# First four tiles of a two-layer attention kernel: another order of work on all five engines, with two large loads moved to ScalarE's queue

## The chip, the cores and the metric

One NeuronCore of a Trainium2 chip runs the kernel alone. The metric is the device time of one execution in microseconds (us); a shorter time is better. The engines are TensorE (PE in the profile, its weight loads PEld), VectorE (DVE), ScalarE (ACT), GpSimd (POOL) and SyncE (SP), which only issues DMAs. ScalarE can issue DMAs too.

## The reference

Two layers of the same form follow each other on x of shape (32, 128, 512). Layer 0 has 16 heads, layer 1 has 8. Cut to what matters:

```python
xn = layernorm(x) * scale + bias
q, k, v = xn @ Wq + bq, xn @ Wk + bk, xn @ Wv + bv      # k and v masked along the sequence
q = softmax(q, over the channels of a head)
k = softmax(k, over the sequence)
att = einsum('bhse,bhsd->bhed', k, v)                   # per head
y = einsum('bhtd,bhed->bhte', q, att)
scale, shift = split(silu(cond) @ film_W + film_b)      # cond is (32, 1024)
h = silu(layernorm(y) * (1 + scale) + shift) @ Wo + bo
x = x + h
```

All is fp32. The kernel splits every operand of a product into a rounded high part and the rest (low part), and sums three products: high by high, high by low, low by high.

## The kernel before

A tile is one of the 64 pairs of layer and batch row (128 positions by 512 channels). Tiles are handled in pairs: `x` is normalised (`stat_x` and `root_x` for mean and deviation, `norm_x`), turned so that the channels lie on the partitions (`turn_x`), scaled (`x_turned`, which writes the high part XH too) and its low part taken (`x_low`). TensorE then makes `keys`, `values` and `queries` (48 matmuls in all), each with the weights' high parts WH (`split_high`) and low parts WL (`split_low`), chunk by chunk of 128 rows. The keys go through mask, maximum and exponential (`keys` on VectorE, `exp_k`, `key_sums`, `normalise_keys`), `attention` forms the product of keys and values, `heads` copies it out of PSUM, `mix` multiplies it with the queries' exponentials (`exp_q`), and `mixed`, `root_y`, `norm_y`, `film`, `h_mul`, `h_high`, `h_low` and `output` do the rest. `conditioning` and `conditioning_fold` make the scales and shifts of all batch rows from `cond`; `conditioning_sums` copies between the two.

For the first two pairs (tiles 0 to 3), `turn_x` is a transpose by TensorE through PSUM. From tile 4 on VectorE transposes blocks of 32 (XS), and two DMAs through DRAM finish it: `write_x` and `read_x` on SP's queue, landing in XT, which `x_turned` reads.

Every engine has its own order of work, written out by hand as a list of calls, and waits on semaphores that its producers raise. The lists of the start (tiles 0 to 4) are written out; `step(s)` repeats from s = 5. An engine does its list strictly in order, so a call that waits holds up all that stand behind it on that engine. SP's list is the order of the DMAs. Weights of layer 0 land in STAGE (keys, later output), and in tiles 8 to 11 and 12 to 15 of X (values, queries), so the loads of those tiles of x come later; the conditioning weights land in tiles 16 to 31 of X.

`keep_busy(b, n)` makes n matmuls of the identity into a PSUM bank whose content nobody reads: two records in the trace for each.

TensorE's list at the start is: 10 `keep_busy`, `turn_x(0)`, `turn_vectors`, `turn_x(1)`, 14 `keep_busy`, `keys(0)`, `keys(1)`, 2 `keep_busy`, `turn_x(2)`, `turn_valid`, `queries(0)`, `values(0)`, `queries(1)`, `turn_x(3)`, `values(1)`, `turn_cond`, `count`, `keys(2)`, `conditioning(0)`, `queries(2)`, `keys(3)`, `values(2)`, `conditioning_fold(0)`, `attention(0)`, `mix(0)`, `attention(1)`, `values(3)`, `queries(3)`, `conditioning(1)`, `mix(1)`, 5 `keep_busy`, `conditioning_fold(1)`, 2 `keep_busy`, `keys(4)`, and so on.

The lines that the prediction names: L1152 the matmuls of `split_product` (keys, values, queries, output), L1232 `attention`, L1248 `mix`, L1305 `turn_x` on TensorE, L1346 `keep_busy`, L1351 `count`; L346 `split_low`, L1575 to L1581 `keys` on VectorE, L1677 the high part of h by a VectorE copy at the end; L687 `mask_of_keys`, L667 `x_low` and L651 `add_bo` on GpSimd; L902 `heads`, L935 and L942 `x_turned`; L405 and L413 `write_x` and `read_x`, L377 and L381 the loads of x and of the weights.

Of the kernel before, what the change touches and what calls it, by code (L numbers as in the profile page):

```python
# [36 lines left out]
P = 128  # L37
# [7 lines left out]
def build_blocks(nc, x, cond, mask0, mask1, weights, film_w, vec_rows, bias_rows, out):  # L45
# [4 lines left out]
    C = D // P  # L50
# [16 lines left out]
    with ctx:  # L67
# [107 lines left out]
        act_cond, act_w = sem("act_cond"), sem("act_w")  # L175
# [164 lines left out]

        def split_low(eng, w, chunks):

            for c in chunks:
                wait_weights(eng, w, c)
                eng.wait_ge(act_w, C * w + c + 1)
                eng.tensor_tensor(WL[w % 4][:, c, :], STAGES[w][:, c, :], WH[w % 4][:, c, :].bitcast(F32),  # L346
                                  ALU.subtract).then_inc(low_w[w][c], 1)
# [26 lines left out]
        def _(eng):  # L374
# [130 lines left out]
            load_bias(2)  # L505
            load_bias(0)
            load_bias(1)
            load_w(2)
            load_film(0)
            load_x(3)  # L510
            wait_split(1)

            load_x(4)
            write_qy(1)
            load_film(1)
# [3 lines left out]
            wait_split(0)  # L519
            load_w(3)  # L520
            write_x(2)
            write_qy(2)
            read_x(2)
            read_qy(2)
            write_qy(3)
            write_x(3)
            masks_at(2)
# [73 lines left out]
        def _(eng):  # L601
# [92 lines left out]
            mask_of_keys(0)  # L694
            root_x(2)
            root_x(3)
            split_low(eng, 2, [0])
            normalise_keys(0)
            queries(0)
            root_x(4)  # L700
            mask_of_keys(1)
            normalise_keys(1)
            root_x(5)
            root_x(6)
            queries(1)
            normalise_keys(2)
            root_x(7)
            root_x(8)
            add_bo(0)
            queries(2)  # L710
            root_x(9)
            add_bo(1)
            root_y(0)
            x_low(4)
            split_low(eng, 3, [1])
            normalise_keys(3)
# [95 lines left out]
        def _(eng):  # L812
# [148 lines left out]

            eng.dma_start(VR, vec_rows).then_inc(ld_vec, 16)
            load_first(eng, [3])
            load_first(eng, [2])
            load_mask(eng, 0)
            eng.dma_start(COND, cond).then_inc(ld_cond, 16)
            eng.dma_start(MI, mask0).then_inc(ld_mask, 16)
            eng.dma_start(MF, mask1).then_inc(ld_mask, 16)
            split_high(0, [0])
            split_high(0, [1])  # L970
            split_high(0, [2])
            split_high(0, [3])
# [4 lines left out]
            cond_tanh()  # L977
            split_high(1, [2])
            split_high(1, [3])
            load_mask(eng, 1)  # L980
# [7 lines left out]
            exp_k(1)  # L988
            norm_x(4)
            exp_k(2)  # L990
            norm_x(5)
            conditioning_sums(0)
            exp_q(0)
            values(0)
            norm_x(6)
            norm_x(7)
            heads(0)
            values(1)
# [3 lines left out]
            values(2)  # L1002
            exp_k(3)
# [3 lines left out]
            heads(1)  # L1007
            exp_q(1)
# [129 lines left out]
        def _(eng):  # L1138
# [229 lines left out]
            keep_busy(B_Q, 4)  # L1368
            keep_busy(B_Q, 6)
            turn_x(0)  # L1370
            turn_vectors()
            turn_x(1)
            keep_busy(B_Q, 2)
            keep_busy(B_Q, 2)
            keep_busy(B_Q, 2)
            keep_busy(B_Q, 2)
            keep_busy(B_Q, 2)
            keep_busy(B_Q, 2)
            keep_busy(B_Q, 2)
            keys(0)  # L1380
            keys(1)
            keep_busy(B_Q, 2)
            turn_x(2)
            turn_valid()
            queries(0)
            values(0)
            queries(1)
            turn_x(3)
            values(1)
            turn_cond()  # L1390
            count()
# [9 lines left out]
            values(3)  # L1401
            queries(3)
            conditioning(1)
            mix(1)
            eng.wait_ge(dve_ka, 4)
            keep_busy(B_K, 5)
            conditioning_fold(1)
            keep_busy(B_K, 2)
# [91 lines left out]
        def _(eng):  # L1500
# [230 lines left out]

            def start():
# [46 lines left out]

            stat_x(0)  # L1780
            stat_x(1)
            norm_x(0)
            split_low(eng, 0, [0])
            norm_x(1)
            split_low(eng, 0, [1])
            split_low(eng, 0, [2])
            start_vectors()
            split_low(eng, 0, [3])
            stat_x(2)
            stat_x(3)  # L1790
            x_low(0)
# [252 lines left out]
```

## Time and profile before

| | us |
|---|---|
| median of three runs | 856.59 (856.27 to 859.33) |
| the profiled execution | 857.14 |
| its span | 855.1 |

The span is the time from the first to the last instruction in the profile. A share of busy time is taken over the whole span. The timeline of an engine lists instructions in order: start, duration, instruction, count and, in brackets, how long the engine sat idle before it and what ended that. The ends of matmuls are modelled and overlap with the next one's start, so on TensorE the starts are what counts.

### The profile page before, as it was taken

To read this page: it belongs to the slowest core of one execution; us is meant where nothing else is said; L and a number is where in the kernel's file an instruction comes from. 1 tells how busy PE (TensorE), PEld (TensorE's weight loads), DVE (VectorE), ACT (ScalarE), POOL (GpSimd) and SP (SyncE) were. 2 spreads that over 40 slices of the span, in tenths; PEclk is the share of its full clock that TensorE was granted. 3 is DMA by queue.
4 is the path that set the end of the run, shared out by engine and by line. 5 is a ranking of instruction groups with operands and counts; after the bars stand their busy time and mean duration, and the time that the engine had idled before them with its cause. 6 is when DMAs were issued, how large, how long until landed. Compare 5 with 4: busy or idle time off the path is not lost.

```text
span 855.1 us, 20095 instructions
## 1 busy us (share of the span) xinstructions
PE 838.2 (98%) x6659; PEld 719.9 (84%) x6659; DVE 679.3 (79%) x1362; ACT 603.1 (71%) x1442; POOL 548.9 (64%) x741
## 2 busy tenths in 40 slices
PE   7999999999999999999999999999999999999998
PEld 7778888888888888888878888888888888888886
DVE  6987778778788788778887887787788787787766
ACT  5376687686676776686876886776776686676665
POOL 3467766766766666766767667667667666765641
PEclk9999999999999999999999999999999999999999
DMA  8876676766667756555587556656566656566441
GB/s 309 286 225 201 201 218 199 228 216 205 195 210 208 233 197 199 179 165 175 169 247 233 185 172 200 201 180 201 179 204 201 202 186 189 178 194 211 142 160 62
DMA packets 139404, 169.81 MB, mean 199 GB/s; under 512 B 12302, under 2 KB 112006, under 8 KB 139302
## 3 DMA queue, kind: packets, MB, share of 16 engines
q1 hardware_dynamic: 138512, 167.56, 62.5%
q8 instruction: 53, 0.87, 0.4%
q10 hardware_dynamic: 790, 0.98, 0.4%
q14 instruction: 49, 0.40, 0.2%
HBM read 95.61 MB, written 72.88 MB: 197 GB/s over the span
## 4 chain that ended last, share of the span: by engine, by line
PE 83%; DMA 6%; DVE 4%; issue 2%; SPq 2%; POOL 1%; ACT 1%; DVEq 0%; POOLq 0%; ACTq 0%
PE PS L1152 72%; PE PS L1248 6%; PE PS L1232 3%; DMA X<-in_x 2%; DMA XT<-x_turned 1%; DMA x_turned<-XS 1%; DMA k_turned<-KT 1%; DMA QT<-qy_turned 1%; POOL XL L667 0%; SPq L400 0%; PE PS L1322 0%; DMA EK<-k_turned 0%; DVE BNX L1515 0%; PE PS L1276 0%; PE PS L1291 0%
## 5 line engine op out<-in xcount | busy, mean ns | idle before, releaser
L680 POOL TENSOR_TENSOR HL<-H,HH 128x512 fp32r<-128x512 f32 x60 | 77.5, 1292 | 185.3 <-ACT HH L916 185.3
L867 ACT ACTIVATE Z<-QT,FC,FA 128x128 f32<-128x128 f32 x240 | 99.0, 483 | 87.7 <-DMA QT<-qy_turned 87.7
L1152 PE MATMUL PS<-XH,WH_k 128*128 128x256 f32 x512 | 149.8, 293 | 0.7 <-DVE KN L1581 0.7
L1152 PE MATMUL PS<-XL,WH_k 128*128 128x256 f32 x512 | 144.8, 283 | 0.0
L1152 PE MATMUL PS<-XH,WL_k 128*128 128x256 f32 x512 | 144.8, 283 | 0.0
L953 ACT ACTIVATE XN<-X,NBX,RSX 128x512 f32<-128x512 f32 x60 | 48.8, 813 | 85.5 <-POOL NBX L629 85.5
L829 ACT ACTIVATE SK<-SK,KN 128x128 f32<-128x128 f32 x256 | 98.9, 387 | 10.7 <-DVE KN L1581 10.4
L1152 PE MATMUL PS<-WH_o,HH 128*128 128x512 f32 x248 | 101.3, 408 | 2.0 <-issue 1.9
L1152 PE MATMUL PS<-WH_v,XH 128*128 128x512 f32 x256 | 100.8, 394 | 0.0
L1152 PE MATMUL PS<-WH_q,XH 128*128 128x512 f32 x256 | 100.7, 393 | 0.0
L1152 PE MATMUL PS<-WL_v,XH 128*128 128x512 f32 x256 | 100.3, 392 | 0.0
L1152 PE MATMUL PS<-WL_q,XH 128*128 128x512 f32 x256 | 99.8, 390 | 0.0
L1152 PE MATMUL PS<-WH_v,XL 128*128 128x512 f32 x256 | 99.6, 389 | 0.0
L1152 PE MATMUL PS<-WH_q,XL 128*128 128x512 f32 x256 | 99.6, 389 | 0.0
L1152 PEld LDWEIGHTS PS<-XH,WH_k 128*128 128x128 f32 x512 | 97.9, 191 | 1.3 <-issue 1.1
L1152 PEld LDWEIGHTS PS<-XL,WH_k 128*128 128x128 f32 x512 | 98.2, 192 | 0.1
L1152 PEld LDWEIGHTS PS<-XH,WL_k 128*128 128x128 f32 x512 | 98.1, 192 | 0.0
L1152 PE MATMUL PS<-WL_o,HH 128*128 128x512 f32 x248 | 96.9, 391 | 0.0
L1152 PE MATMUL PS<-WH_o,HL 128*128 128x512 f32 x248 | 96.9, 391 | 0.0
L651 POOL TENSOR_TENSOR X<-X,BB 128x512 f32<-128x512 f32 x64 | 83.8, 1311 | 0.2
L667 POOL TENSOR_TENSOR XL<-XF,XH 128x512 fp32r<-128x512 f32 x60 | 78.1, 1302 | 5.2 <-issue 3.6
L674 POOL TENSOR_TENSOR SK<-SK,RE 128x512 f32<-128x512 f32 x64 | 66.8, 1044 | 19.7 <-DVE RE L1587 19.6
(171 smaller groups left out, 2106.6 us busy)
## 6 DMA issues: line engine op xcount, KB each, us to landing
qy_turned<-QS SPq DMA_DIRECT2D x60, 512.0 KB, 2.9
QT<-qy_turned SPq DMA_DIRECT2D x240, 128.0 KB, 3.1
EK<-k_turned SPq DMA_DIRECT2D x128, 128.0 KB, 2.8
x_turned<-XS SPq DMA_DIRECT2D x30, 512.0 KB, 3.3
XT<-x_turned SPq DMA_DIRECT2D x120, 128.0 KB, 3.5
k_turned<-KT SPq DMA_DIRECT2D x52, 256.0 KB, 3.8
out_x<-X SPq DMA_DIRECT2D x31, 256.0 KB, 3.2
X<-in_x SPq DMA_DIRECT2D x11, 512.0 KB, 5.3
```

The lines of the kernel that those rows point to most:

```text
L651: eng.tensor_tensor(X[:, b, :], X[:, b, :], BB[:, 2, :], ALU.add).then_inc(pool_bo, 1)
L667: eng.tensor_tensor(XL[g % 2][:, dst, :], XF0[:, :, :], XH[g % 2][:, dst, :].bitcast(F32), ALU.subtract).then_inc(pool_xl, 1)
L674: eng.tensor_tensor(sk, sk, RE[:, :].unsqueeze(2).to_broadcast([P, 4, T]), ALU.mult).then_inc(pool_kn, 1)
L680: eng.tensor_tensor(hl_of(o), h_of(o), hh_of(o).bitcast(F32), ALU.subtract).then_inc(pool_hl, 1)
L829: e = eng.activation(SK[:, p, a, :], SK[:, p, a, :], ACT.Exp, bias=KN[:, p, t, cc:cc + 1], accum_out=SE[:, p, a:a + 1])
L867: z = eng.activation(z_of(o)[:, c * P:c * P + P].rearrange("p (q n) -> p q n", q=Q), src, ACT.Identity, bias=FC[l][:, c, b:b + 1], scale=F ...
L953: eng.activation(XN[:, t, :], X[:, n % B, :], ACT.Identity, bias=NBX[:, r:r + 1], scale=RSX[:, r:r + 1]).then_inc(act_xn, 1)
L1152: mm = eng.matmul(dst, left[a](c), right[b](c), start=(c == 0 and a + b == 0), stop=(c == C - 1 and a == 1))
L1232: mm = eng.matmul(PS[f:f + 32, bank_att(j), c * P + a:c * P + a + w], vs if l == 0 else ks, ks if l == 0 else vs, start=True, stop=True, t ...
L1248: mm = eng.matmul(bank(B_Y + c // 2, (c % 2) * W, W), EQ[:, c * P:c * P + P], ATT[:, c // 2, (c % 2) * W:(c % 2 + 1) * W], start=True, sto ...
```

## The change

Nothing is computed otherwise; what changes is the order of the start, which engine does some of its steps, and how much `keep_busy` there is:

- ScalarE's queue no longer issues the mask and `cond` loads; SP does, behind the load of the values' weights. ScalarE issues instead the second conditioning load and the output weights' load (2 MB and 1 MB), after `exp_k(1)`. SP had issued them behind `write_qy(1)` and behind `place_keys(0)`.
- Two of the four high parts of the keys' weights are made by VectorE, one low part of each of the keys', values' and queries' weights moves from VectorE to GpSimd.
- `start` and `start_vectors` move to the front of VectorE's list; TensorE turns the vectors first.
- TensorE turns tiles 2 and 3 together ahead of the first projections, takes values before queries, and `conditioning(1)` before `queries(3)`.
- On ScalarE `heads(1)` and `exp_q(1)` go ahead of the copies of the output weights and of `x_turned(4)`; on GpSimd `add_bo(1)` moves behind `x_low(4)`, in front of `x_low(5)`.
- 25 `keep_busy` instead of 24 stand ahead of `keys(0)`; the other nine behind it are gone.

```diff
@@ -172,7 +172,7 @@
 pe_fold, act_cp = sem("pe_fold"), sem("act_cp")
-act_cond, act_w = sem("act_cond"), sem("act_w")
+act_cond, act_w, dve_w = sem("act_cond"), sem("act_w"), sem("dve_w")
 act_ek, act_eq, act_z, act_t = sem("act_ek"), sem("act_eq"), sem("act_z"), sem("act_t")
@@ -338,11 +338,20 @@
+def wait_high(eng, w, c):
+    if w == 0 and c >= C // 2:
+        eng.wait_ge(dve_w, c - C // 2 + 1)
+    elif w == 0:
+        eng.wait_ge(act_w, c + 1)
+    else:
+        eng.wait_ge(act_w, C * w - C // 2 + c + 1)
 def split_low(eng, w, chunks):
...
         wait_weights(eng, w, c)
-        eng.wait_ge(act_w, C * w + c + 1)
+        wait_high(eng, w, c)
         eng.tensor_tensor(WL[w % 4][:, c, :], STAGES[w][:, c, :], WH[w % 4][:, c, :].bitcast(F32),
@@ -502,29 +511,30 @@
     load_w(1)
-    load_bias(2)
+    load_mask(eng, 0)
+    eng.dma_start(MI, mask0).then_inc(ld_mask, 16)
+    eng.dma_start(MF, mask1).then_inc(ld_mask, 16)
+    eng.dma_start(COND, cond).then_inc(ld_cond, 16)
+    load_w(2)
     load_bias(0)
     load_bias(1)
-    load_w(2)
     load_film(0)
+    load_mask(eng, 1)
     load_x(3)
     wait_split(1)
     load_x(4)
     write_qy(1)
-    load_film(1)
     write_keys(0)
...
     place_keys(0)
-    wait_split(0)
-    load_w(3)
+    load_bias(2)
+    write_qy(2)
     write_x(2)
-    write_qy(2)
+    read_qy(2)
     read_x(2)
-    read_qy(2)
+    masks_at(2)
+    write_x(3)
     write_qy(3)
-    write_x(3)
-    masks_at(2)
     read_qy(3)
@@ -691,29 +701,32 @@
     root_x(1)
-    mask_of_keys(0)
+    split_low(eng, 0, [3])
     root_x(2)
     root_x(3)
+    split_low(eng, 1, [3])
+    mask_of_keys(0)
     split_low(eng, 2, [0])
+    split_low(eng, 2, [1])
     normalise_keys(0)
+    mask_of_keys(1)
     queries(0)
+    normalise_keys(1)
     root_x(4)
-    mask_of_keys(1)
-    normalise_keys(1)
     root_x(5)
+    queries(1)
     root_x(6)
-    queries(1)
     normalise_keys(2)
     root_x(7)
+    queries(2)
+    add_bo(0)
     root_x(8)
-    add_bo(0)
-    queries(2)
     root_x(9)
-    add_bo(1)
     root_y(0)
     x_low(4)
+    normalise_keys(3)
     split_low(eng, 3, [1])
-    normalise_keys(3)
+    add_bo(1)
     x_low(5)
@@ -959,25 +972,29 @@
+    def load_output():
+        for c in range(C):
+            eng.wait_ge(low_w[0][c], 1)
+        eng.dma_start(STAGE[:, :, :], weights[0][3].rearrange("(c p) n -> p c n", p=P)).then_inc(ld_w[2], 16)
+    def load_second_film():
+        l, a, k = FILM_STEPS[1]
+        eng.dma_start(FILM0[:, :, a:a + k], film_w[l].rearrange("(k p) n -> p k n", p=P)[:, :, a:a + k])                   .then_inc(ld_film[1], 16)
     eng.dma_start(VR, vec_rows).then_inc(ld_vec, 16)
+    load_first(eng, [2])
     load_first(eng, [3])
-    load_first(eng, [2])
-    load_mask(eng, 0)
-    eng.dma_start(COND, cond).then_inc(ld_cond, 16)
-    eng.dma_start(MI, mask0).then_inc(ld_mask, 16)
-    eng.dma_start(MF, mask1).then_inc(ld_mask, 16)
     split_high(0, [0])
     split_high(0, [1])
-    split_high(0, [2])
-    split_high(0, [3])
     x_turned(0)
...
     split_high(1, [1])
-    cond_tanh()
     split_high(1, [2])
     split_high(1, [3])
-    load_mask(eng, 1)
+    cond_tanh()
     split_high(2, [0])
@@ -986,26 +1003,28 @@
     exp_k(1)
+    load_second_film()
+    load_output()
     norm_x(4)
-    exp_k(2)
     norm_x(5)
     conditioning_sums(0)
+    exp_k(2)
+    values(0)
+    values(1)
     exp_q(0)
-    values(0)
     norm_x(6)
+    heads(0)
+    exp_k(3)
     norm_x(7)
-    heads(0)
-    values(1)
+    values(2)
+    heads(1)
+    exp_q(1)
     split_high(3, [0])
...
     split_high(3, [2])
-    values(2)
-    exp_k(3)
     norm_y(0)
...
     norm_x(8)
-    heads(1)
-    exp_q(1)
     x_turned(5)
@@ -1365,30 +1384,23 @@
     eng.wait_ge(pool_const, 2)
-    keep_busy(B_Q, 4)
-    keep_busy(B_Q, 6)
+    keep_busy(B_Q, 10)
+    turn_vectors()
+    keep_busy(B_Q, 1)
     turn_x(0)
-    turn_vectors()
     turn_x(1)
-    keep_busy(B_Q, 2)
-    keep_busy(B_Q, 2)
-    keep_busy(B_Q, 2)
-    keep_busy(B_Q, 2)
-    keep_busy(B_Q, 2)
-    keep_busy(B_Q, 2)
-    keep_busy(B_Q, 2)
+    keep_busy(B_Q, 14)
     keys(0)
     keys(1)
-    keep_busy(B_Q, 2)
     turn_x(2)
+    turn_x(3)
     turn_valid()
+    values(0)
     queries(0)
-    values(0)
+    values(1)
+    count()
     queries(1)
-    turn_x(3)
-    values(1)
     turn_cond()
-    count()
     keys(2)
@@ -1399,13 +1411,10 @@
     values(3)
+    conditioning(1)
     queries(3)
-    conditioning(1)
     mix(1)
-    eng.wait_ge(dve_ka, 4)
-    keep_busy(B_K, 5)
     conditioning_fold(1)
-    keep_busy(B_K, 2)
     def step(s):
@@ -1729,6 +1738,12 @@
+    def split_high(w, chunks):
+        for c in chunks:
+            wait_weights(eng, w, c)
+            eng.tensor_copy(WH[w][:, c, :], STAGES[w][:, c, :]).then_inc(dve_w, 1)
     def start():
@@ -1777,74 +1792,73 @@
+    start()
     stat_x(0)
...
     norm_x(0)
+    start_vectors()
+    norm_x(1)
+    split_high(0, [2])
+    split_high(0, [3])
     split_low(eng, 0, [0])
-    norm_x(1)
     split_low(eng, 0, [1])
     split_low(eng, 0, [2])
-    start_vectors()
-    split_low(eng, 0, [3])
+    x_low(0)
+    x_low(1)
     stat_x(2)
     stat_x(3)
-    x_low(0)
-    x_low(1)
     split_low(eng, 1, [0])
-    start_masks()
     norm_x(2)
+    split_low(eng, 1, [1])
     norm_x(3)
...
     keys(0)
-    split_low(eng, 2, [1])
+    start_masks()
     split_low(eng, 2, [2])
-    split_low(eng, 1, [3])
     split_low(eng, 2, [3])
-    split_low(eng, 1, [1])
+    start_valid()
     keys(1)
     key_sums(0)
-    queries(0)
-    stat_x(4)
     values(0)
-    turn_queries(0)
-    stat_x(5)
-    stat_x(6)
-    start()
-    start_cond()
     x_low(2)
     x_low(3)
-    start_valid()
+    queries(0)
+    start_cond()
     turn_keys(0)
     key_sums(1)
+    turn_queries(0)
+    turn_keys(1)
+    values(1)
     start_cond_turned()
     queries(1)
-    turn_keys(1)
+    stat_x(4)
+    stat_x(5)
     zero_attention()
     keys(2)
-    values(1)
     start_count()
...
     turn_x(4)
+    turn_x(5)
     key_sums(2)
-    turn_x(5)
+    stat_x(6)
+    queries(2)
     stat_x(7)
+    keys(3)
+    values(2)
     stat_x(8)
     stat_x(9)
-    queries(2)
-    values(2)
-    keys(3)
     mixed(0)
+    conditioning(0)
     turn_queries(2)
-    conditioning(0)
     turn_x(6)
+    turn_x(7)
     split_low(eng, 3, [0])
...
     split_low(eng, 3, [2])
-    turn_x(7)
-    queries(3)
     turn_keys(2)
...
     values(3)
+    queries(3)
     mixed(1)
```

## Rows read from the trace of the kernel before

**Rows 1.** The profile's page, first part: busy time by engine.
```profile
PE 838.2 (98%) x6659; PEld 719.9 (84%) x6659; DVE 679.3 (79%) x1362; ACT 603.1 (71%) x1442; POOL 548.9 (64%) x741
```
**Rows 2.** Busy time by stretch: stretch, length, engines, granted TensorE clock, DMA share, GB/s.
```profile
7.00:8.00 1.00, 0.03 (x1) 0.00 (x0) 0.00 (x0) 0.99 (x2) 0.00 (x0) 1.00 0.76 181
...
13.00:14.00 1.00, 1.00 (x6) 1.00 (x6) 0.93 (x3) 0.97 (x3) 0.28 (x2) 1.00 1.05 406
...
130.00:400.00 270.00, 269.63 (x2162) 231.53 (x2161) 216.99 (x439) 194.30 (x467) 179.38 (x243) 1.00 0.66 203
```
**Rows 3.** TensorE's timeline: start, duration, instruction, count, idle before and its releaser.
```profile
9.87 0.69 PE L1305 MATMUL PS<-ident,XN 128*128 128x128 f32 x2 [2.84 <-DVE XN L1526]
...
15.97 0.36 PE L1152 MATMUL PS<-XH,WH_k 128*128 128x256 f32 x1
...
23.01 0.50 PE L1152 MATMUL PS<-WH_q,XH 128*128 128x512 f32 x1
...
36.14 0.41 PE L1351 MATMUL PS<-VALID,H 128*128 128x32 f32 x2 [0.72 <-DVE VALID L1749]
...
50.66 0.46 PE L1232 MATMUL PS<-EK,VV 128*32 128x32 f32 x32
...
61.48 1.17 PE L1248 MATMUL PS<-ATT,EQ 128*128 128x132 f32 x8 [0.51 <-ACT EQ L847]
62.49 1.28 PE L1346 MATMUL PS<-ident 128*128 128x128 f32 x10
...
64.97 0.36 PE L1152 MATMUL PS<-XH,WH_k 128*128 128x256 f32 x1
```
**Rows 4.** L1346 by group, first in 11.7 to 13.5 us, then in 14.5 to 16.
```profile
L1346 PE MATMUL PS<-ident 128*128 128x128 f32 x9 | 2.1, 421 | 0.0
...
L1346 PE MATMUL PS<-ident 128*128 128x128 f32 x16 | 2.0, 277 | 0.0
```
**Rows 5.** VectorE's timeline around the first tile's keys.
```profile
19.12 0.69 DVE L1575 TENSOR_TENSOR SK<-PS,MB 128x512 f32<-128x512 f32 x1 [0.31 <-PE PS L1152]
...
20.57 1.02 DVE L1579 TENSOR_TENSOR KB<-KM,VC 128x4 f32<-128x4 f32 x1
```
**Rows 6.** GpSimd's timeline.
```profile
10.77 1.40 POOL L687 TENSOR_SCALAR MB<-MB 128x256 f32<-128x256 int32 x1 [4.07 <-DMA MB<-in_mask]
...
20.28 1.29 POOL L346 TENSOR_TENSOR WL_q<-X,WH_q 128x512 fp32r<-128x512 f32 x1 [4.33 <-ACT WH_q L819]
...
52.24 1.28 POOL L651 TENSOR_TENSOR X<-X,BB 128x512 f32<-128x512 f32 x1
...
59.87 1.30 POOL L667 TENSOR_TENSOR XL<-XF,XH 128x512 fp32r<-128x512 f32 x1 [3.55 <-issue]
...
63.34 1.28 POOL L667 TENSOR_TENSOR XL<-XF,XH 128x512 fp32r<-128x512 f32 x1
```
**Rows 7.** ScalarE's timeline: weight copies, first `heads`, `norm_y`, `x_turned(4)`.
```profile
19.48 2.20 ACT L819 ACTIVATE WH_q<-X 128x512 fp32r<-128x512 f32 x4 [0.87 <-DMA X<-in_wq]
...
51.20 0.60 ACT L902 ACTIVATE ATT<-PS 128x512 f32<-128x512 f32 x1 [3.20 <-PE PS L1232]
...
56.35 0.82 ACT L836 ACTIVATE YN<-YN,NBY,RSY 128x512 f32<-128x512 f32 x1 [0.24 <-POOL NBY L639]
57.97 1.09 ACT L935 ACTIVATE XF<-XT,VC 128x256 f32<-128x256 f32 x2 [0.81 <-DMA XT<-x_turned]
59.10 0.63 ACT L942 ACTIVATE XH<-XF 128x512 fp32r<-128x512 f32 x1
```
**Rows 8.** Issue to landing, first 60 us: weight loads (L381), then loads of x (L377).
```profile
DMA to landing us min/median/max: 7.1/11.7/11.7
...
DMA to landing us min/median/max: 2.9/6.9/17.6
```
**Rows 9.** SP's timeline: the x write to DRAM of tiles 4, 5, its four reads.
```profile
45.05 0.50 SPq L405 DMA_DIRECT2D x_turned<-XS  x1
...
53.01 1.84 SPq L413 DMA_DIRECT2D XT<-x_turned  x4
```

## The prediction

> **What bounds the kernel now.** I read the page first: TensorE is busy 838 of 855 us [rows 1], and from 130 to 400 us it has under half a microsecond of idle time [rows 2]. So after the start the time is TensorE's work. Nothing of that work changes, and whatever the start gives or takes is carried to the end. The bookmark is the first matmul of `keys(4)`: it begins at 64.97 us [rows 3], and behind it TensorE has the same list in both kernels. My forecast is the shift of that bookmark, at 1 us per us.
>
> Then I read the start on TensorE's timeline [rows 3]. Three kinds of time could go. First, the head: TensorE waits 2.84 us for the second tile's `norm_x` and reaches `keys(0)` at 15.97. Second, waits behind it: 0.72 us at `count`, 0.51 at `mix(1)`. Third, the nine late `keep_busy`: ten records from 62.49 take 1.28 us. The other eight records go too, so 18 records at about 0.12 us are 2.2 us. The question is whether these stand in waits that would be there anyway. For the last seven the answer is in GpSimd's timeline: `x_low(5)`, which `keys(4)` needs, starts at 63.34 and ends at 64.62 [rows 6], 0.35 us ahead of `keys(4)`. They filled a wait, and taking them out alone gives nothing. So the chain to follow is the one that makes tiles 4 and 5.
>
> **Part 1, up to the first projection.** The first matmul behind `keys(1)`'s group is at 23.01 before [rows 3]. After, TensorE could be there sooner: `norm_x(1)` no longer stands behind a weight part that waits for ScalarE, so the 2.84 us wait goes, and the fourteen `keep_busy` end near 12 to 13 instead of 15.97. But `keys(0)` at 12.5 and the two tiles' 5.8 us (the 7.0 from 15.97 to 23.01 less two dummies and two small steps) end TensorE's keys near 18.3, the turned tiles 2 and 3 near 19, and then `turn_valid` waits for `start_masks`, which VectorE now has behind `keys(0)`. VectorE's `keys(0)` needs GpSimd's `mask_of_keys(0)`, which stands behind `split_low(1, [3])`, which needs the values' weights. That chain sets the first projection:
> - The values' weights landed at most 11.7 us after their issue near 3.05, at 14.75 [rows 8]. Ahead of them the mask and `cond` loads of ScalarE's queue (0.3 MB, 0.7 us at 406 GB/s) go, and a microsecond in which only 181 GB/s moved [rows 2] may fill up. I take 13.3, between 12.5 and 14.75.
> - ScalarE's four copies, 2.2 us [rows 7]: 15.5. GpSimd's low part 1.29 and mask 1.40 [rows 6]: 18.2.
> - VectorE's `keys(0)`. Before, it took 2.5 us from 19.12 to the end of its third operation at 21.59, plus 0.2 for the last. That third one, 128x4, took 1.02 us and ended with GpSimd's low part, which ran from 20.28 to 21.57 [rows 5, 6]. Held up like that `keys(0)` takes 2.7 us; with 0.16 for the 128x4 it takes 1.8. After, GpSimd takes two low parts of the queries' weights just then, so I take 2.7: 20.9. The mask rows and two small transposes add 0.4: first projection at 21.3.
>
> The Trainium skill (SBUF — State Buffer, "SBUF: two separate sides") says that a VectorE instruction with two SBUF inputs and a GpSimd instruction share a port pair as an exclusive lock held for the whole instruction. The 1.02 us row agrees. Without the lock the first projection would be at 20.4 and the kernel 0.9 us faster than I say.
>
> The bounds: landing at 12.5 and no hold-up, 19.6; landing at 14.75 with it, 22.7.
>
> **Part 2, to `attention(0)`.** Before, 27.65 us lie between 23.01 and 50.66 [rows 3]. After, the same matmuls follow, without `turn_x(3)` (0.4 us, now ahead) and without the `count` wait (0.72 and its issue, 0.8): 26.4, so 47.7. The order of values and queries costs nothing. What could wait: `queries(1)` needs VectorE's `queries(0)`, near 28.5 against 30; `keys(3)` needs VectorE's `keys(2)`, near 40 against 41. VectorE is nearly full from 21 to 47, so this is the thinnest cover; each microsecond that VectorE is later than that costs up to one.
>
> **Part 3, to `keys(4)`.** Before, ScalarE starts `heads(0)` at 51.20, 0.54 behind `attention(0)`, and ends `x_turned(4)` at 59.73, having waited 0.81 for the DMA and 0.24 for GpSimd [rows 7]. After, the same stretch holds `heads(1)`, `exp_q(1)` and a `norm_x` more and one `values` less, all of 128x512 (the shown ones of this size take 0.55 to 0.8 with 0.1 of overlap: 0.5 + 0.5 + 0.7 - 0.6), and no wait: 8.5 - 1.05 + 1.1 = 8.5 us. The DMA wait goes, since before the write of tiles 4 and 5 was issued at 45.05, right behind the 1 MB output weights, and its reads could go out only at 53.01 [rows 9]; now the weights are issued by ScalarE some 10 us earlier. So `x_turned(4)` ends at 47.7 + 0.5 + 8.5 = 56.7. GpSimd took from 59.87 to 64.62 for `x_low(4)`, a low part, the normalising and `x_low(5)`, 4.75 us; now `add_bo(1)`, 1.28 us, stands among them [rows 6]. That is 56.85 + 4.75 + 1.27 = 62.85, and 0.35 more for TensorE: `keys(4)` at 63.2 instead of 64.97, 1.8 us sooner. TensorE itself would be ready at about 59.8 (second rival), so it idles some 3 us, in place of the dummies.
>
> The moves with one answer: the two VectorE copies and `start` lie in waits of the first 8 us; the two loads on ScalarE's queue hold its sequencer some microseconds where ScalarE would wait for `norm_x(4)` anyway; `load_bias(2)` is needed only by `add_bo(0)`, 9 us later.
>
> **The sum.** 857.14 - 1.8 = 855.3 against the profiled execution, which is 0.55 above the median of the runs. From the median: 856.6 - 1.8 = **854.8 us**. With the bounds of part 1 it is 853.1 to 856.2.
>
> **Rivals.**
> - *TensorE's own work sets `keys(4)`.* From `attention(0)` to `keys(4)` before are 14.31 us [rows 3], less fourteen dummy records (1.7) and the 0.51 wait: 12.1. So 47.7 + 12.1 = 59.8, 5.2 us sooner: 851.4, and 849.7 with the early bound of part 1. For it: ScalarE's and GpSimd's orders could overlap better than my walk, and GpSimd waits long ahead of `x_low(4)` now (3.55 us). Against it: 15 us of ScalarE and GpSimd work in series behind `heads(0)`, counted from rows.
> - *The idle time slows TensorE down.* The same dummy took 421 ns a record in 11.7 to 13.5 us, about 4 us after TensorE resumed behind 2.84 us of idleness, and 277 ns in 14.5 to 16 [rows 4], though the granted clock column says 1.00 throughout [rows 2]. That is the 1.2 and the 2.4 GHz level. Before it, the engine had been slow as well, so no row shows that some 3 us of nearly idle time bring the slow level. If they do, 4 us of work at half speed cost 2 us: 856.8. The Trainium skill (TensorE: Matmul & The Clock Gate, "What's actually happening") has the array fall back to half rate when idle; it speaks against taking out the seven dummies ahead of `keys(4)`.
> - *Slower: the mask rows land late.* They go out behind 1 MB of weights on SP's queue, near 7.3 us. On that queue loads took up to 17.6 us to land [rows 8]. TensorE's `turn_valid` waits for them with all projections behind it. From a landing past 23 us each microsecond is one on the end; at 17.6 us after issue they land at 24.9, the first projection is at 25.2 and the kernel 3.9 us behind the forecast, 2.1 slower than before: 858.7. Against it: that longest landing was a load behind 2 MB more, and the masks are small.
> - *It doesn't do what it says.* VectorE is the fuller engine from 21 to 47 us and gives the lead back; `keys(4)` stays within a microsecond: 856.6.
>
> **Chances.** Forecast 0.46, TensorE's own work 0.28, slow clock 0.10, late masks 0.07, no effect 0.09. The range of 80% is 850.6 to 858.0: it leaves out most of the late masks and the early end of the first rival. Half a per cent, about what a measurement of this kernel can tell from no change, is 4.3 us. Faster than 852.3 is most of the first rival and the forecast's tail: 0.25. Slower than 860.9 would need masks or a load later still: 0.05. The same: 0.70.
>
> **What would show it.** `keys(0)` near 12.5 us and an idle TensorE ahead of the first projection, ended by VectorE; the first projection at 21.3; `attention(0)` near 47.7; no DMA wait ahead of `x_turned(4)`; an idle TensorE ahead of `keys(4)` ended by GpSimd's `x_low(5)`; `keys(4)` at 63.2, and from there equal distances. If `keys(4)` is at 60 the first rival holds. If the matmuls of `keys(4)` lie 0.24 us apart rather than 0.12, it is the clock. The prediction is wrong if stalls of another place, such as `step(5)` and on, differ between the kernels.

## The result, and the profile after

| | before | after |
|---|---|---|
| median of 17 runs each, us | 857.74 (855.94 to 861.16) | 862.07 (858.83 to 864.03) |
| ratio, 95% interval | | 1.0045 (1.0033 to 1.0057) |
| profiled execution, us (span) | 857.14 (855.1) | 861.16 (859.4) |

The changed kernel is about 3.9 us slower, where I had forecast 1.8 faster and a range that ended at 858.0. Half a per cent, the line I had drawn for "the same", is 4.3 us, so the ratio lies just inside it; but its interval leaves out 1, and the slowdown is real.

First part of the page of after, busy time by engine. It answers [rows 1]: TensorE has nearly as many microseconds of work, though 16 dummy records fewer (the nine late `keep_busy` are 18 records, the one more ahead of `keys(0)` two).

```profile
PE 837.5 (97%) x6643; PEld 718.7 (84%) x6643; DVE 682.1 (79%) x1361; ACT 602.4 (70%) x1440; POOL 553.3 (64%) x744
```

TensorE's timeline of after (start, duration, instruction, count, idle before and its releaser), for [rows 3]. In order: the fourteen `keep_busy`, `keys(0)`, `turn_valid`, the values of tile 0 with their first, second and eighth matmul, the first queries, `attention(0)`, the end of `mix(1)`, `conditioning_fold(1)`, `keys(4)` and its twelfth matmul, and the queries behind it.

```profile
8.04 3.29 PE L1365 MATMUL PS<-ident 128*128 128x128 f32 x28
12.64 0.35 PE L1171 MATMUL PS<-XH,WH_k 128*128 128x256 f32 x1 [1.31 <-DVE XL L1572]
...
22.11 0.41 PE L1383 MATMUL PS<-ident,QS 32*128 32x32 f32 x2 [2.55 <-DVE QS L1759]
22.45 0.80 PE L1171 MATMUL PS<-WH_v,XH 128*128 128x512 f32 x1
23.05 0.63 PE L1171 MATMUL PS<-WL_v,XH 128*128 128x512 f32 x1
...
25.47 0.39 PE L1171 MATMUL PS<-WL_v,XH 128*128 128x512 f32 x1
...
26.63 0.40 PE L1171 MATMUL PS<-WH_q,XH 128*128 128x512 f32 x1
...
50.08 0.46 PE L1251 MATMUL PS<-EK,VV 128*32 128x32 f32 x32
...
60.49 1.06 PE L1267 MATMUL PS<-ATT,EQ 128*128 128x132 f32 x8
63.19 1.08 PE L1351 MATMUL PS<-FOLD,Z 128*128 128x32 f32 x8 [1.64 <-ACT Z L924]
65.83 0.35 PE L1171 MATMUL PS<-XH,WH_k 128*128 128x256 f32 x1 [1.56 <-POOL XL L677]
...
67.95 0.41 PE L1171 MATMUL PS<-XH,WL_k 128*128 128x256 f32 x1
...
70.26 0.39 PE L1171 MATMUL PS<-WH_q,XH 128*128 128x512 f32 x1
```

The head is as forecast: `keys(0)` begins at 12.64 instead of 15.97. By `attention(0)` the lead is only 0.58 us (50.08 against 50.66), and `keys(4)` is 0.86 late (65.83 against 64.97). Both groups behind the idle stretches are long. The values of tile 0 take from 22.45 to 26.63, 4.2 us; those of tile 2 in the same profile (46.43 to 49.18) take 2.75. `keys(4)` takes from 65.83 to 70.26, 4.4 us, where the two groups of keys before it take 3.1 and 2.9. Their 128x512 matmuls take 0.63 us instead of 0.39, the 128x256 0.41 instead of 0.28. The stretches of one microsecond say why. The columns are the stretch, its length, TensorE's busy time and matmul count, the granted clock, the DMA share and GB/s:

```profile
21.00:22.00 1.00, 0.00 (x0) 0.94 1.04 403
22.00:23.00 1.00, 0.89 (x3) 0.50 1.07 402
...
24.00:25.00 1.00, 1.00 (x4) 0.50 1.05 410
25.00:26.00 1.00, 1.00 (x5) 0.85 1.06 410
...
66.00:67.00 1.00, 1.00 (x7) 0.63 0.63 142
67.00:68.00 1.00, 1.00 (x7) 0.50 0.00 0
68.00:69.00 1.00, 1.00 (x6) 0.50 0.77 319
69.00:70.00 1.00, 1.00 (x8) 0.66 0.51 205
70.00:71.00 1.00, 1.00 (x8) 1.00 0.05 4
```

Twice the granted clock falls to 0.50 (1.2 GHz) just as dense work resumes, and stays there some 3.4 us. The time lost is the sum of one minus the clock: 0.06 + 3 x 0.50 + 0.15 = 1.7 us, and 0.37 + 0.50 + 0.50 + 0.34 = 1.7 us. In the profile of before, the same windows show 1.00.

I profiled each kernel twice more. In the three profiles of before, `keys(4)` begins on average at 64.96 us and `keys(5)` at 78.37, in the three of after at 64.92 and 80.46. So on average `keys(4)` is not late: the 0.86 us are that one profile's, and what after loses up to `keys(5)`, 2.1 us, arises in between, where the slow clock is. The further steps are the same list of matmuls, and yet the distance from there to the last output group is not quite the same: to the fifth group -0.15 us, over the next 22 groups +0.3, over the change of layer (groups 26 to 32) +1.35, over the last stretch +0.8. I come back to that at the end.

### The profile page after: what moved, and what is told of

Same layout as the page of the kernel before. It is cut to its first block, busy times and chain, and to the rows that moved or that the text cites. A ratio compares the mean times of both kernels' runs of the same rounds, so it can differ in the third digit from the quotient of the medians.

```text
span 859.4 us, 20063 instructions
## 1 busy us (share of the span) xinstructions
PE 837.5 (97%) x6643; PEld 718.7 (84%) x6643; DVE 682.1 (79%) x1361; ACT 602.4 (70%) x1440; POOL 553.3 (64%) x744
## 4 chain that ended last, share of the span: by engine, by line
PE 80%; DMA 4%; DVE 3%; issue 2%; POOL 2%; ACT 1%; SPq 1%; DVEq 0%; POOLq 0%; ACTq 0%
PE PS L1171 70%; PE PS L1267 6%; PE PS L1251 3%; DMA qy_turned<-QS 1%; DMA QT<-qy_turned 1%; DMA k_turned<-KT 1%; DMA EK<-k_turned 1%; POOL XL L677 1%; POOL SK L684 0%; PE PS L1341 0%; POOL HL L690 0%; SPq L447 0%; PE PS L1295 0%; PE PS L1310 0%; DVE BNY L1671 0%
```

## The experiments

The theory: what costs is not the wait alone but the slow clock behind it, some 1.7 us each time. The seven dummies ahead of `keys(4)` had kept the clock up; the change takes the filling away, or leaves a new wait unfilled. The rivals: the start is late on VectorE or GpSimd (their new order), the loads moved to another queue cost something, or a later start grows on the way.

Each ratio is to the kernel before, timed in the same series: its median there was 857.81 us for the runs with dummies put in or taken out, 859.60 for the orders and the loads, 858.10 for the repeats and the two last attempts, 859.06 for the later start. The place of `keys(4)` and `keys(5)` is that of one profiled execution each.

Every execution, profiled or not, also has a mean granted clock on record. Over a span of 860 us a mean of 0.998 is 1.7 us lost, 0.996 is 3.4. Before isn't free of it: in 113 executions of these four series 25 are at 1.000, 52 at 0.998 and 36 at 0.996, 1.9 us on average. After has 4.4 us on average in 27 (17 first and 10 of the repeat), 25 of them at 0.996 or lower. The difference is 2.5 us.

**Two repeats.** A fresh run of each kernel shows what a profile and a timing vary by.

> The kernel before itself, for a second profile. Its first profile had two steps behind keys(5) that were half a microsecond longer than in the other kernels. If those are chance, its keys(4) is again near 65 and output(4) about 1 us earlier than in the first profile, so that the changed kernel's loss at the start is 2.3 us rather than 1.3; if they belong to the kernel, they are there again. Ratio 1.000 either way.

> The changed kernel itself, for a second profile. Clock theory: the two waits of 2.6 and 1.6 + 1.6 us and the two stretches at granted clock 0.50 are there again, keys(4) within 0.7 of 65.8; ratio 1.0045. If the slow stretches were chance, they lie elsewhere or are missing.

Measured: before 857.15 us, 0.9993 (0.9976 to 1.0010), and after 862.53, 1.0050 (1.0034 to 1.0066). The slowdown stands. One spell of slow clock (1.7 us between 9 and 13 us) was in this profile of before too, among the dummies ahead of `keys(0)`; after's repeat has one between 8 and 12. So a spell early in the start comes and goes with the execution. It costs before little: `keys(0)` begins at 15.29 there, and at 15.03 in before's third profile, which has no spell. Over the 113 executions those at 0.996 are only 0.8 us longer than those at 1.000, not 3.4. In after's repeat `turn_valid` waited only 1.30 us, and there the clock stayed up. Ahead of `keys(4)` the waits were as in the first profile (1.60 and 1.55 us), but 3.4 us were lost instead of 1.7.

**Dummies back in the new order, at both places, then at one.** The edit, on after:

```diff
             turn_x(3)
+            keep_busy(B_Q, 10)
             turn_valid()
...
             mix(1)
+            eng.wait_ge(dve_ka, 4)
+            keep_busy(B_K, 6)
             conditioning_fold(1)
+            keep_busy(B_K, 6)
```

> The changed kernel with ten dummies in the wait ahead of turn_valid and six and six around conditioning_fold(1). Clock theory: the waits stay as long, but the granted clock stays at 1.00; the first twelve values matmuls take 2.7 us instead of 4.2, those of keys(4) 2.9 instead of 4.4. keys(4) starts at 64.4 and keys(5) at 77.7 instead of 80.7; ratio to the kernel before 1.001 (between 0.999 and 1.003). Order theory (the two longer chains are the whole loss): no change against the changed kernel, ratio 1.0045.

Measured 858.07 us, 1.0003 (0.9987 to 1.0018). Nothing is computed with these dummies, and they make the kernel 0.4% faster than after: 862.07 to 858.07. TensorE's timeline of this kernel at the second place, and its stretches:

```profile
61.16 1.08 PE L1351 MATMUL PS<-FOLD,Z 128*128 128x32 f32 x8 [0.29 <-ACT Z L924]
62.08 1.58 PE L1365 MATMUL PS<-ident 128*128 128x128 f32 x12
63.71 0.36 PE L1171 MATMUL PS<-XH,WH_k 128*128 128x256 f32 x1
...
66.66 0.40 PE L1171 MATMUL PS<-WH_q,XH 128*128 128x512 f32 x1
```

```profile
65.00:66.00 1.00, 1.00 (x11) 1.00 0.00 0
66.00:67.00 1.00, 1.00 (x9) 1.00 0.78 311
```

`keys(4)` takes 2.95 us at clock 1.00 instead of 4.4. At the first place the values of tile 0 take 21.78 to 24.64, 2.9 us instead of 4.2. And it isn't this profile alone: all twelve executions have a mean granted clock of 1.000, where after's 17 average 0.995.

> Dummies only ahead of turn_valid. Clock theory: the first slow spell goes, the second stays; keys(4) starts at 64.4 and is still slow, keys(5) at 79.2; ratio 1.0027. Order theory: 1.0045.

Only the ten: 859.74 us, 1.0019 (1.0004 to 1.0033). The profile keeps 1.00 at the first place and loses 3.4 us between 60 and 70; the twelve executions average 0.997.

> Dummies only around conditioning_fold(1). Clock theory: the first slow spell stays, keys(4) starts at 65.8 at full clock, keys(5) at 79.1; ratio 1.0027. Order theory: 1.0045.

Only the six and six: 859.07 us, 1.0005 (0.9990 to 1.0020). Here the 1.7 us between 20 and 26 stay, and the second place is at full clock. The twelve average 0.998. The ratio is lower than the 1.0027 that I expected, and its interval leaves that out. Each place is worth about half or more of the loss; how much each, these intervals don't part. With the both-places run, that is what the theory says, and no other engine's order was touched.

**The dummies out of before.**

```diff
             mix(1)
-            eng.wait_ge(dve_ka, 4)
-            keep_busy(B_K, 5)
             conditioning_fold(1)
-            keep_busy(B_K, 2)
```

> The kernel before without the wait and the seven dummies ahead of keys(4). Clock theory: TensorE idles some 2.2 us there in two pieces, near the 2.6 us that brought the slow clock in the changed kernel; if it falls, keys(4) takes 4.4 us and the ratio is 1.0018; if two pieces of a microsecond are too short, the ratio is 1.000. Order theory: 1.000, since the dummies only filled a wait that x_low(5) ends.

Measured 860.77 us, 1.0033 (1.0017 to 1.0048). This is the part of the change that I had costed at nothing. Its timeline and stretches:

```profile
60.90 1.17 PE L1248 MATMUL PS<-ATT,EQ 128*128 128x132 f32 x8 [0.95 <-ACT EQ L847]
63.03 1.08 PE L1332 MATMUL PS<-FOLD,Z 128*128 128x32 f32 x8 [0.97 <-ACT Z L911]
64.27 0.36 PE L1152 MATMUL PS<-XH,WH_k 128*128 128x256 f32 x1 [0.16 <-issue]
...
68.70 0.40 PE L1152 MATMUL PS<-WH_q,XH 128*128 128x512 f32 x1
```

```profile
64.00:65.00 1.00, 0.84 (x6) 0.89 1.00 245
65.00:66.00 1.00, 1.00 (x7) 0.50 0.99 236
...
67.00:68.00 1.00, 1.00 (x6) 0.50 0.62 258
68.00:69.00 1.00, 1.00 (x9) 0.90 0.65 266
```

`keys(4)` starts no later than in the three profiles of before (64.25 to 65.67), and takes 4.4 us. Two waits of 0.95 and 0.97 us, with eight small matmuls of `mix(1)` and eight of the fold around them, were enough. The profile has a second spell, 1.7 us between 10 and 14, like before's repeat. But it doesn't account for the whole 0.33%, some 2.9 us: `keys(5)` is at 79.12, 0.75 later than in before on average, and the rest of this execution's loss lies behind it.

**VectorE's order.** The mask rows ahead of the keys, on after:

```diff
             split_low(eng, 1, [2])
-            keys(0)
             start_masks()
+            keys(0)
```

> The changed kernel with start_masks one place ahead of keys(0) on VectorE. The 2.55 us wait ahead of turn_valid goes and with it the first slow spell: values(0) starts at 19.9 instead of 22.45 and takes 2.7 us. Theory that VectorE's order behind it is not a bound: attention(0) at 46.2 instead of 50.1, keys(4) at 61.9, there still slow; keys(5) at 76.7, ratio 1.000. Rival (VectorE is full from 20 to 47 us and is the next bound): attention(0) at 48, keys(4) near 64, ratio 1.0025.

Measured 860.85 us, 1.0015 (0.9998 to 1.0031). `turn_valid` waits for nothing, the first projection is at 19.47 and `attention(0)` at 47.13. So the 2.55 us wait was `start_masks` behind `keys(0)`. But the 2.95 us of `attention(0)` shrink to 0.94 at `keys(4)` (64.89), since ScalarE and GpSimd can't follow (the profiled execution, 864.48 us, is the slowest of the twelve, so its waits may be long):

```profile
62.35 1.08 PE L1351 MATMUL PS<-FOLD,Z 128*128 128x32 f32 x8 [3.06 <-ACT Z L924]
64.89 0.55 PE L1171 MATMUL PS<-XH,WH_k 128*128 128x256 f32 x1 [1.47 <-POOL XL L677]
```

TensorE now idles 4.5 us there in two pieces, and 3.4 us are lost to the slow clock; `keys(4)` takes 5.3. The wait was moved rather than removed. VectorE is late in three places (0.39, 0.42 and 0.64 us).

**GpSimd's order.** `add_bo(1)` back ahead of `root_y(0)`, on after:

```diff
             root_x(9)
+            add_bo(1)
             root_y(0)
             x_low(4)
             normalise_keys(3)
             split_low(eng, 3, [1])
-            add_bo(1)
             x_low(5)
```

> The changed kernel with add_bo(1) back ahead of root_y(0) on GpSimd. x_low(5) ends 1.27 us earlier, so keys(4) starts at 64.5 instead of 65.8. Clock theory: the 1.64 us wait ahead of conditioning_fold(1) stays and the next shrinks to 0.3; the kernel before without its dummies fell to half clock behind two waits of 0.95, so this falls too: keys(5) at 79.4, ratio 1.003. Rival (only the wait counts, or the clock stays up): 77.9, ratio 1.0015.

Measured 861.90 us, 1.0031 (1.0014 to 1.0048). `keys(4)` is at 64.52, 1.3 us sooner than in after's first profile, and its wait is 0.34 instead of 1.56; the fold still waits 1.58, and the clock falls all the same. The idle time was shortened, and nothing clear of the noise came of it.

**All of it together:** masks early, `add_bo(1)` early, and dummies at the second place (5 and 4), the one where a long wait was left.

> The changed kernel with start_masks early, add_bo(1) early, and five and four dummies around conditioning_fold(1). If slow clock and the two long chains are the whole loss: attention(0) at 46.2, keys(4) at 60.7 at full clock, keys(5) at 74; 4 us less than the kernel before, ratio 0.995. If VectorE bounds: keys(4) near 62.5, ratio 0.998.

Measured 858.04 us, 0.9979 (0.9959 to 0.9999). That it beats before isn't shown: before's median was 859.60 us in this series and 857.7 to 859.1 in the others, and the next two kernels, which hold all of this one, also measure 858.0 and come out level (0.9996 and 1.0000). It is faster than after. `attention(0)` is at 46.60 and the clock holds, in all twelve executions at a mean of 1.000:

```profile
53.78 1.92 PE L1341 MATMUL PS<-X,CT 128*32 128x512 f32 x16 [1.44 <-DVE FA L1735]
...
61.15 1.08 PE L1351 MATMUL PS<-FOLD,Z 128*128 128x32 f32 x8 [0.44 <-ACT Z L924]
62.06 1.14 PE L1365 MATMUL PS<-ident 128*128 128x128 f32 x8
62.95 0.36 PE L1171 MATMUL PS<-XH,WH_k 128*128 128x256 f32 x1
```

Two attempts to take more followed, each on top of the one above. The first puts `x_turned(4)` ahead of `norm_y(0)` on ScalarE, the second also puts `conditioning(1)` behind `queries(3)` on TensorE.

> The kernel with masks and add_bo(1) early and nine dummies, and x_turned(4) ahead of norm_y(0) on ScalarE. ScalarE waited 1.3 us for norm_y(0) there. If ScalarE's series behind heads(0) is the bound: x_turned(4) starts at 54 instead of 55.6, x_low(5) and keys(4) up to 1.5 earlier, keys(4) at 61.5, ratio 0.996. Rival (norm_y(0) later holds up turn_y and key_sums on VectorE, which normalise_keys(3) ahead of x_low(5) waits for): no gain, ratio 0.998.

Measured 858.00 us, 0.9996 (0.9980 to 1.0013), `keys(4)` at 62.33.

> As the one before, with conditioning(1) behind queries(3) on TensorE again. TensorE waited 1.4 us for VectorE's conditioning(0) ahead of it. If that wait counts: keys(4) another 0.5 to 1 earlier, ratio 0.995. Rival (x_low(5) sets keys(4)): the wait only moves, ratio as the one before.

Measured 858.03 us, 1.0000 (0.9988 to 1.0011), `keys(4)` at 63.14. The 1.44 us ahead of `conditioning(1)` came back as 1.64 at the fold. Neither gives anything that can be told from nothing. This profile has its 1.7 us of slow clock elsewhere, from 460 us on, at the change of layer, behind a single wait of 1.76 us:

```profile
458.82 0.65 PE L1251 MATMUL PS<-VV,EK 128*32 128x64 f32 x32 [1.76 <-DMA EK<-k_turned]
```

**The loads alone.** On before, only the second film part and the output weights leave SP's list and go out on ScalarE's queue behind `exp_k(1)`. The edit in short, with the engine in brackets:

```diff
-            load_film(1)                (SP)
-            wait_split(0)               (SP)
-            load_w(3)                   (SP)
+            load_second_film()          (ScalarE, behind exp_k(1))
+            load_output()               (ScalarE)
```

> The kernel before with only the two large loads moved to ScalarE behind exp_k(1). My step (the move takes the DMA wait ahead of x_turned(4) away): the write of tiles 4 and 5 at 45 lands in 3.3 us instead of 8, x_turned(4) starts 0.8 us earlier, x_low(5) at 63.8, dummies fill the rest, keys(4) at 64.4; ratio 0.9995. Rival (ScalarE is held up by the issue, or the transfers collide with the writes of keys and queries): attention(0) later, ratio 1.002.

Measured 861.82 us, 1.0023 (1.0006 to 1.0040). The DMA wait ahead of `x_turned(4)` is gone: SP could send the reads of the x write at 51.43 instead of 53.01 [rows 9]. But the 3 MB now move beside small reads of the other queue (L438, the turned queries, 64 KB each), and those took 5.0 us in the median and 7.3 at most to land, where before they took 2.1 and 3.4. ScalarE waits for them, and `attention(0)` for the turned keys:

```profile
47.06 0.63 ACT L844 ACTIVATE EQ<-QT 128x512 f32<-128x512 f32 x1 [3.53 <-DMA QT<-qy_turned]
```

```profile
50.36 0.46 PE L1242 MATMUL PS<-EK,VV 128*32 128x32 f32 x32 [0.87 <-DMA EK<-k_turned]
51.59 1.44 PE L1258 MATMUL PS<-ATT,EQ 128*128 128x132 f32 x8 [0.77 <-ACT ATT L899]
...
53.55 0.80 PE L1162 MATMUL PS<-WH_v,XH 128*128 128x512 f32 x1
54.15 0.63 PE L1162 MATMUL PS<-WL_v,XH 128*128 128x512 f32 x1
```

and behind these 0.87 + 0.77 us the clock is at 0.50 once more, 1.7 us lost (and 1.7 between 7 and 12, in the head). `attention(0)` isn't later than in before (50.26 to 50.66), and the profiled execution, 858.15 us, is the fastest of its twelve, so that these waits make the 0.23% is likely and not shown. In after the loads go out sooner (26.4 and 27.0 us, here 32.5 and 33.1), and neither wait is there.

**A later start.** Before, with 40 more dummies ahead of `keys(4)` (`keep_busy(B_K, 42)`), asks whether a delay grows on the way to the end.

> The kernel before with 40 dummies more ahead of keys(4), 40 x 0.245 = 9.8 us of TensorE work at full clock. Step tested: a shift of keys(4) is carried to the end one to one. Then keys(5) moves by 9.8 us (some of it less if dummies fill waits) and the ratio is 1.0114. Rival (a late start costs more later, at the change of layers or in the second half, which would explain why the changed kernel's ratio of 1.0045 is 1.5 to 2 us above the shift at keys(5)): 1.016 or more, with the surplus in the stretch from output(26) to output(32) or behind it. Other rival (later stretches give some back): under 1.010.

Measured 866.58 us, 1.0086 (1.0058 to 1.0114), that is 7.4 us for a start that is 9.4 late at `keys(5)` (87.78 against 78.37). It is carried and not amplified. Whether a little of it is taken up, the interval (5.0 to 9.8 us) doesn't say. Nor are the 9.4 us all dummies: the profile also has a slow spell from 36.8 to 40.4 us, in `keys(2)`, behind waits of 0.50 and 0.72 us.

**One look more at each kernel**, for the stretches behind the start.

> The kernel before, third profile, to see how far its distances between outputs differ by chance: output(4) to output(26) 282.1 and 282.6 us so far, output(26) to output(32) 80.9 and 79.7, output(32) to the last 356.1 and 357.0. If the second half is longer in the changed kernel by nature, this one stays at or under 357.

> The changed kernel, third profile. So far output(26) to output(32) 82.5 and 81.2 us, output(32) to the last 357.3 and 358.3. If these 1 to 1.5 us over the kernel before are its own, they are there again; if chance, they scatter into the range of the kernel before.

Measured 858.79 and 861.86 us. After's profile again loses 1.7 us between 22 and 28 and 3.4 between 64 and 72; before's has `keys(5)` at 79.06, after's at 81.05. Over the change of layer before has 80.4 us and after 81.4; in the last stretch it is 357.3 in before, over the 357 that I had set, and 357.2 in after. Before's profile shows one thing more, which no theory here had: TensorE waits 2.46 us ahead of `keys(0)`, and 1.60 at `mix(1)` with its dummies right behind, and loses nothing to the clock. The clock stays at 1.00, and the matmuls of `keys(0)` soon lie 0.12 us apart.

```profile
15.03 0.36 PE L1152 MATMUL PS<-XH,WH_k 128*128 128x256 f32 x1 [2.46 <-DVE XL L1563]
15.22 0.28 PE L1152 MATMUL PS<-XL,WH_k 128*128 128x256 f32 x1
...
62.18 1.17 PE L1248 MATMUL PS<-ATT,EQ 128*128 128x132 f32 x8 [1.60 <-ACT EQ L847]
```

## Why the prediction was wrong, point by point

**What bounds the kernel:** right in the main. Later starts end later. But "from there equal distances" doesn't hold to the microsecond: from `keys(5)` to the end the 17 profiles of these kernels show 775.8 to 781.8 us.

**The head and the keys:** `keys(0)` at 12.5, measured 12.64 (11.97 and 13.29 in the repeats). By luck in part: the dummies end at 11.33, not at 12 to 13, and `keys(0)` waits another 1.31 us for VectorE's `x_low`. TensorE then idles ahead of `turn_valid`, and VectorE's `start_masks` ends the wait: right, 2.55 us.

**The first projection:** forecast at 21.3, measured at 22.45. The weights landed as I took it (copies from 13.33) and `mask_of_keys(0)` ended at 19.25 where my sum had 18.2. VectorE's and GpSimd's timelines of after show why:

```profile
16.73 1.55 DVE L1535 TENSOR_SCALAR XN<-X,MVX,RSX 128x512 f32<-128x512 f32 x1
...
19.35 0.69 DVE L1584 TENSOR_TENSOR SK<-PS,MB 128x512 f32<-128x512 f32 x1 [0.26 <-POOL MB L697]
...
20.80 0.93 DVE L1588 TENSOR_TENSOR KB<-KM,VC 128x4 f32<-128x4 f32 x1
```

```profile
16.71 1.29 POOL L355 TENSOR_TENSOR WL_v<-X,WH_v 128x512 fp32r<-128x512 f32 x1
18.09 1.16 POOL L697 TENSOR_SCALAR MB<-MB 128x256 f32<-128x256 int32 x1
19.22 2.49 POOL L355 TENSOR_TENSOR WL_q<-X,WH_q 128x512 fp32r<-128x512 f32 x2
```

GpSimd's low part could begin only at 16.71, behind `root_x` steps that I had not put into the sum, and not when ScalarE's copies ended at 15.5. The hold-up that I had taken (0.93 us for the 128x4, while GpSimd's low parts run) came. So did one that I hadn't: `norm_x(3)` took 1.55 us beside a low part of GpSimd, and 0.54 us a microsecond before. The size was off by 1.15 us, within my bounds.

**To `attention(0)`:** forecast 26.4 us from the first projection, measured 27.6. The rows give the difference: 1.4 us of half clock in the values of tile 0. No wait for VectorE came, as I had said.

**To `keys(4)`:** ScalarE from `heads(0)` to the end of `x_turned(4)` 8.74 us (50.62 to 59.36; forecast 8.5), without a DMA wait. GpSimd from `x_low(4)` to the end of `x_low(5)` 5.97 us (59.50 to 65.47; forecast 4.75 + 1.27), its last step:

```profile
64.19 1.28 POOL L677 TENSOR_TENSOR XL<-XF,XH 128x512 fp32r<-128x512 f32 x1
```

`keys(4)` 0.36 behind it (forecast 0.35). These were the thick terms of the sum, and they held. TensorE idled 1.64 + 1.56 = 3.2 us, as I had said ("some 3 us"). (The rival that this sentence of the prediction calls the second is the first of its list.)

**The step that failed** is the sentence on the dummies: "They filled a wait, and taking them out alone gives nothing." It gives a loss, 0.33% (0.17 to 0.48). I had priced idle time of TensorE by its length alone, and idle time can have a second part behind it: the three profiles of after have 3.4 us or more at the two places together, and with both places filled the executions are 3.7 us shorter in the mean (858.3 against 862.0). This was in the prediction as the second rival, with about the right size (2 us; rows show 1.7 or 3.4) and the right sign to look for (matmuls of keys farther apart; they lie 0.21 us apart at the slow clock, not the 0.24 that I wrote, and 0.12 at the full one). But I gave it 0.10, and only at one place. The new wait ahead of `turn_valid`, which I had forecast myself, is 2.55 us, not much shorter than those ahead of `keys(4)` together. The Trainium skill (TensorE: Matmul & The Clock Gate, "What's actually happening") has the array fall back when idle; the runs agree, at clock 0.50 and 1.7 us a time, though not each time. I had [rows 4] as a possible sign of it, and set it aside because the engine had been slow before that wait too; the slow dummies there also lie 1.8 to 3.6 us behind the first matmul after the wait, not about 4. Before's repeat has the same 421 ns a dummy with the column at 0.50.

**The size of the miss.** The forecast was 854.8 us and the median is 862.07, 7.3 more. Before's own median was 1.15 higher in the 17 executions than in the first three; `keys(4)` is 1.7 us later than forecast (64.92 on average against 63.2); 2.1 arise between `keys(4)` and `keys(5)`, and 2.2 behind `keys(5)`.

**The other rivals.** TensorE's own work didn't set `keys(4)`. The mask rows landed in time: 7.4 us after their issue at 5.7, and 8.0 after 6.4. `keys(4)` did stay within a microsecond of before, as the last rival had it, but not because "VectorE gives the lead back": that doesn't hold in after, and it holds in part once the start is sooner (waits of 0.41, 0.44 and 1.44 us with all of it together). "The same" in the sense of half a per cent, which I had given 0.70, is where the ratio lies, but not for a reason of mine.

**The loads** I had called free in after's place. In after, where they leave at 26.4 us, no wait of TensorE in the start is ended by them; what they cost there wasn't measured alone. Sent some 6 us later, on before, they cost 0.23%.

**What stays open.** After loses 3.9 us. The dummies bring back 3.6 between the ratios (1.0045 to 1.0003) and 3.3 between the places of `keys(5)` (80.46 to 77.15), and with them no execution shows slow clock. So the slow clock is the dearest part of after's start, and filling its waits takes the loss away. It isn't the whole difference between the two kernels, though: before loses 1.9 us to the slow clock itself, on average and cheaply, and the kernel with both dummies, which loses none, is only level with it.

The profiles put only 2.1 us at `keys(5)`. Some 2 us more appear behind it, most at the change of layer (81.70 against 80.35 us on average, three profiles each) and in the last stretch (357.6 against 356.8), where after shows no slow clock. For the last stretch this may be chance: kernels that differ only in the start show 357.2 to 359.2. At the change of layer there is a pattern. The seven profiles with slow clock at `keys(4)` have 81.2 to 82.8 us there; of the ten without it nine have 79.7 to 81.3, and the tenth, 81.9, has its slow spell in this very stretch. After's order with both dummies belongs to the low ones (80.9), before's order without its seven to the high ones (82.0). So in these profiles the surplus goes with the slow clock at `keys(4)` rather than with the order. I saw this only afterwards, and what would carry it over 340 us isn't shown; one late start of 9.4 us didn't bring it (81.1). Nor is shown how the loss parts between the two places.

## What to carry to other kernels

A wait on TensorE costs its length and can cost 1.7 or 3.4 us of half clock behind it, so price both. Where filler follows the wait, as in before's head, the slow clock cost far less in the end. Matmuls that compute nothing, set into a wait, are then not dead weight, and shortening the wait without ending it gave nothing clear here. Before filler is deleted, look for what stands in its place when it is gone, and where a reordering opens a new wait, fill it or move what ends it (here two lines on VectorE). Look at the mean clock of every execution, of the kernel before too: one profile at 1.00 doesn't speak for the rest. Moving bulk loads to another queue frees the queue but not the engines behind it: ask which small reads are under way at that time.

## What the hardware showed that I had not expected

- Two waits of 0.95 and 0.97 us with small matmuls between them were followed by a clock of 0.50 and 1.7 us lost; so were 0.87 and 0.77, 1.58 and 0.34, and 2.55 in one piece. Nor is length alone what decides: single waits of 2.39, 2.49 and 2.52 us in the head of before and its variants were followed by it, one of 2.46 us ahead of `keys(0)` wasn't; one of 1.76 us at the change of layer was, those of 1.30, 1.44 and 1.60 us (this one with filler behind it) weren't; and 0.50 and 0.72 us around small matmuls were, once. No run here shows what decides.
- The loss came as 1.7 us or as 3.4, and as nothing between. Waits of the same length (1.64 + 1.56, 1.60 + 1.55, 1.63 + 1.46 us ahead of `keys(4)`) cost 1.7 in one profile of after and 3.4 in the two others.
- A VectorE instruction with one 128x512 input from SBUF and per-partition scalars took 1.55 us beside a GpSimd low part and 0.54 right before it, so the hold-up isn't kept to the two-input form of [rows 5]. The Trainium skill (SBUF — State Buffer, "SBUF: two separate sides") lets VectorE take the shared pair in two cases, with two SBUF inputs or in a mode that uses both ports; the second would cover this row, but no run here shows which mode it was in.
- Small reads on one queue took 5.0 us in the median beside 3 MB of weights on another, and 2.1 before; the four of them that went out while both loads were under way took 6.5 to 7.3.
